# Adding the output projection's bias by an accumulating DMA instead of a thirteenth matmul

## The reference, cut to what matters

```python
qkv = x @ W_attn + b_attn
attn = softmax(masked(k q / sqrt(32)))        # 8 batches x 16 heads, 1024 x 1024
out = combine(attn, v)                        # 8 x 1024 x 512
x = layernorm(x + (out @ W_out + b_out))      # the part that changes: + b_out
scores = x @ w_router                         # top half of the tokens
x = layernorm(x + scatter(sigmoid(scores) * (gelu(x_sel @ W1 + b1) @ W2 + b2)))
```

## Time and profile before

| | |
|---|---|
| median of 3 runs | 2532.54 us (2531.82 to 2533.45) |
| span of the profiled execution | 2531.8 us; the page gives no time around it, the median is 0.7 above it |
| mean granted TensorE clock | 0.990 |
| PE busy | 2456.4 us (97%) |
| POOL busy | 1568.4 us (62%) |
| DVE busy | 1658.1 us (65%) |
| ACT busy | 1191.0 us (47%) |
| the attention alone, 127 to 1700 us | PE 1538.0 of 1573.0 us, POOL 1277.2, DVE 1149.2, ACT 943.9 |
| the feed-forward block, from 1860 us | PE 659.1 of 671.8 us, POOL 154.3 |

### The profile page before, as it was taken

One profiled execution on the slowest core, in us unless ns is written; L12 is line 12 of the kernel. 1 busy time (PEld: TensorE's weight loads), 2 busy tenths in 40 slices (PEclk: granted clock), 3 DMA queues, 4 the chain that ended last, 5 costly groups with the idle time before them and its releaser, 6 DMA issues. The chain is left out here.

```text
span 2531.8 us, 40908 instructions
## 1 busy us (share of the span) xinstructions
PE 2456.4 (97%) x14168; PEld 1817.1 (72%) x14168; DVE 1658.1 (65%) x4230; ACT 1191.0 (47%) x2035; POOL 1568.4 (62%) x1642
## 2 busy tenths in 40 slices
PE   8999999999999999999999999997999999999997
PEld 6656676767777677777767667774788888888886
DVE  7767677677767777767787776775655544553533
ACT  3665566556566656656656565566521111111110
POOL 2878778788888788878788887875233122221311
PEclk9999999999999999999999999998999999999999
DMA  4233445335344433535434343443421001010000
GB/s 175 89 127 120 146 141 195 123 127 182 125 147 158 153 134 136 172 131 177 146 124 159 123 172 128 158 146 102 162 80 35 24 26 43 25 34 26 26 25 17
DMA packets 167502, 287.45 MB, mean 114 GB/s; under 512 B 23241, under 2 KB 58121, under 8 KB 166026
## 3 DMA queue, kind: packets, MB, share of 16 engines
q1 hardware_dynamic: 160130, 267.99, 30.2%
q0 software_dynamic: 7168, 16.85, 2.1%
HBM read 116.97 MB, written 65.11 MB: 72 GB/s over the span
## 5 line engine op out<-in xcount | busy, mean ns | idle before, releaser
L867 POOL TENSOR_TENSOR Pa<-Pa,Pm 128x512 f32<-128x512 f32 (+1 forms) x602 | 744.8, 1262 | 105.8 <-ACT Pm L982 92.4
L1492 PE MATMUL PS<-Qp,Kp 128*128 128x512 f32 (+3 forms) x1536 | 488.8, 354 | 23.4 <-ACT Pm L982 13.1
L1458 PE MATMUL PS<-Kp,Qp 128*128 128x512 f32 (+3 forms) x1536 | 487.4, 352 | 9.1 <-DVE nm L1082 6.4
L982 ACT ACTIVATE Pm<-PS 128x512 f32<-128x512 f32 (+1 forms) x643 | 358.3, 569 | 264.7 <-PE PS L1492 219.4
L1082 DVE TENSOR_REDUCE nm<-PS 128x1 f32<-128x512 f32 x512 | 344.8, 688 | 188.0 <-PE PS L1458 187.7
L867 POOL TENSOR_TENSOR Pa<-Pa,P 128x512 f32<-128x512 f32 (+1 forms) x297 | 368.5, 1265 | 51.0 <-ACT P L982 44.4
L1458 PEld LDWEIGHTS PS<-Kp,Qp 128*128 128x128 f32 x1536 | 278.0, 190 | 110.0 <-issue 34.8
L1492 PEld LDWEIGHTS PS<-Qp,Kp 128*128 128x128 f32 x1536 | 278.0, 190 | 102.9 <-ACT Pa L982 28.9
L1090 DVE CUSTOM_DVE_ANT_0 PS<-PS,maskA 128x384 f32<-128x384 f32 (+3 forms) x512 | 246.4, 509 | 151.4 <-PE PS L1458 150.3
L944 ACT ACTIVATE G<-PS,b1c 128x512 f32<-128x512 f32 x128 | 88.2, 689 | 539.6 <-PE PS L1545 539.6
L1090 DVE CUSTOM_DVE_ANT_0 PS<-PS,maskA,nm 128x384 f32<-128x384 f32 (+3 forms) x512 | 265.1, 554 | 87.6 <-PE PS L1458 83.3
(11 more groups left out here) (149 smaller groups left out, 4229.2 us busy)
## 6 DMA issues: line engine op xcount, KB each, us to landing
Qp<-nat SPq DMA_DIRECT2D x192, 256.0 KB, 2.5
Kp<-nat SPq DMA_DIRECT2D x192, 256.0 KB, 2.9
o_s<-Of SPq DMA_DIRECT2D x64, 256.0 KB, 2.2
Ot<-o_s SPq DMA_DIRECT2D x64, 256.0 KB, 3.0
xb<-in_x SPq DMA_DIRECT2D x64, 256.0 KB, 3.0
h_s<-hs SPq DMA_DIRECT2D x64, 256.0 KB, 2.4
out<-xb SPq DMA_DIRECT2D x64, 256.0 KB, 2.4
x_raw<-in_xt SPq DMA_DIRECT2D x15, 1024.0 KB, 6.3
```

The lines of the kernel that those rows point to most:

```text
L867: e.tensor_tensor(to, to, probs(u, k)[:, h0:h0 + many, 0:w], ALU.add).then_inc(s["padd"], many)
L982: e.activation(probs(u, k)[:, hh[0]:hh[-1] + 1, 0:w], tile_bank(j)[:, 0:len(hh) * w].rearrange("p (h n) -> p h n", n=w), ACT.Exp).then_inc ...
L1458: ins = e.matmul(to, Qp[:, u % 4, h_, qt * P:qt * P + P], Kp[:, (2 * i + k0 // 512) % 4, h_, 0:w], start=True, stop=True)
L1492: ins = e.matmul(tile_bank(j)[:, x_ * w:x_ * w + w], Kp[:, (2 * i + k // 4) % 4, h_, k % 4 * P:k % 4 * P + P], Qp[:, u % 4, h_, 512 - w:51 ...
```

## The change

The thirteenth piece of O goes. CB becomes a full tile of 128 rows that all hold crow: once, after job C, SP stores crow to DRAM and loads it back to all partitions. For each O tile POOL issues one DMA that adds CB to xb in SBUF (128 x 512 float32, 256 KB), four beats after the load of xb at its place in the order, or one beat ahead of the tile's last piece where that is earlier. POOL waits for the load before it, DVE waits for it before line 1160. With 12 pieces T.beat of the O jobs 0 to 54 is one beat smaller, so that all that follows them in the order stands one beat earlier; for O number 55 to 63 it stays. The loads of xb keep their beats. SP's load of b2B, which reuses the memory, waits for all the additions.

```diff
-PIECES = {"K": [1] * 12, "Q": [1] * 12, "V": [1] * 12, "O": [1] * 13, ...
+PIECES = {"K": [1] * 12, "Q": [1] * 12, "V": [1] * 12, "O": [1] * 12, ...
-        CB = sb("CB", [P, D], F32R)
+        CB = sb("CB", [P, D], F32)
+        o_add = {}
+        for load in o_load:
+            for j in o_load[load]:
+                o_add.setdefault(min(load + 4, T.beat[j] - 1), []).append(j)
# sync
+                if n == T.beat["C",] + 2:
+                    e.wait_ge(*freed(("C",)))
+                    e.dma_start(cD[:, :], crow).then_inc(s["cb_st"], 16)
+                if n == T.beat["C",] + 5:
+                    e.wait_ge(s["cb_st"], 16)
+                    e.dma_start(CB[:, :], cD[0].rearrange("(a n) -> a n", a=1).broadcast_to([P, D])).then_inc(s["cb_in"], 16)
...
                     ff_load(7)
+                    for k in range(2):
+                        e.wait_ge(s["x_bias", k], 16 * len(T.o_jobs) // 2)
# gpsimd
-            e.memset(CB[:, :].bitcast(F32), 0.0).then_inc(s["ones"], 1)
...
                         layer_norm(o)
+                for j in o_add.get(n, ()):
+                    o = o_number(j)
+                    if o == 0:
+                        e.wait_ge(s["cb_in"], 16)
+                    e.wait_ge(s["xb", o % 2], 16 * (o // 2 + 1))
+                    e.dma_start(xb[:, o % 2, :], CB[:, :], accum_op=ALU.add).then_inc(s["x_bias", o % 2], 16)
# vector, job C
-                    link(e.tensor_tensor(crow, src[0:1, :], crow, ALU.add))
-                    linked()
-                    link(e.tensor_copy(CB[0:1, :], crow))
-                    linked()
-                    e.tensor_tensor(CB[96:97, :], crow, CB[0:1, :].bitcast(F32), ALU.subtract).then_inc(s["ev_v"], 1)
+                    e.tensor_tensor(crow, src[0:1, :], crow, ALU.add).then_inc(s["ev_v"], 1)
# vector, job O
-                    e.wait_ge(s["xb", o % 2], 16 * (o // 2 + 1))
+                    e.wait_ge(s["x_bias", o % 2], 16 * (o // 2 + 1))
# tensor, job O
-                    if k < 12:
-                        ins = e.matmul(to, Os[:, oh, kt, :], Wo[wh][:, kt, :], start=k == 0, stop=False)
-                    else:
-                        ins = e.matmul(to, ones[0:97, :], CB[0:97, :], start=False, stop=True)
+                    ins = e.matmul(to, Os[:, oh, kt, :], Wo[wh][:, kt, :], start=k == 0, stop=k == 11)
```

More of the change, by code:

```diff
@@ L157, in dense_jobs @@
     return jobs
-PIECES = {"K": [1] * 12, "Q": [1] * 12, "V": [1] * 12, "O": [1] * 13, "T": [2], "S": [1], "N": [4], "C": [4] * 4}
+PIECES = {"K": [1] * 12, "Q": [1] * 12, "V": [1] * 12, "O": [1] * 12, "T": [2], "S": [1], "N": [4], "C": [4] * 4}
 TICKS = 54
@@ L472, in layer @@
         bA, sc, sg = cs["battn"], cs["sc"], cs["sg"]
-        hD, scD, wD, oD = dr["h"], dr["sc"], dr["wqkv"], dr["o"]
+        hD, scD, wD, oD, cD = dr["h"], dr["sc"], dr["wqkv"], dr["o"], dr["cb"]
         xr = x.rearrange("b (t p) d -> b t p d", p=P)
@@ L1267, in vector @@
                     e.wait_ge(s["c0"], 9)
-                    e.wait_ge(s["ones"], 2)
+                    e.wait_ge(s["ones"], 1)
                     e.wait_ge(s["rk0"], 1)
@@ L1370, in wait_ready @@
                         e.wait_ge(s["wo_lo"], 2)
-                        e.wait_ge(*freed(("C",)))
                 if d >= 2:
@@ L1414, in dense @@
                 elif kind == "O":
-                    if k < 12:
-                        term, kt = divmod(k, KT)
-                        oh, wh = ((0, 0), (1, 0), (0, 1))[term]
-                        ins = e.matmul(to, Os[:, oh, kt, :], Wo[wh][:, kt, :], start=k == 0, stop=False)
-                    else:
-                        ins = e.matmul(to, ones[0:97, :], CB[0:97, :], start=False, stop=True)
+                    term, kt = divmod(k, KT)
+                    oh, wh = ((0, 0), (1, 0), (0, 1))[term]
+                    ins = e.matmul(to, Os[:, oh, kt, :], Wo[wh][:, kt, :], start=k == 0, stop=k == 11)
                 elif kind == "N":
@@ L1621 @@
 SEMAPHORES = ("c0", "bias", "b_scaled", "wq_in", "w1_in", "x0_hi", "rk0", "w_in", "w_hi", "w_split", "w_st", "v_in", "v_hi", "v_split", "v_st", "wo_in",
-              "wo_hi", "wo_lo", "x_hi", "x_lo", "ones", "rows", "d_mm", "ev_v", "ev_a", "kq_hi", "a_mm", "a_max",
+              "wo_hi", "wo_lo", "cb_st", "cb_in", "x_hi", "x_lo", "ones", "rows", "d_mm", "ev_v", "ev_a", "kq_hi", "a_mm", "a_max",
               "shift", "b_mm", "b_exp", "keep", "padd", "pv", "o_cp", "nln", "rinv", "ot", "os_hi", "os",
@@ L1626 @@
               "ghi", "glo", "dn", "q_clear", "k_ones")
-SLOTTED = {"xraw": 2, "of_st": 2, "nat": 2, "ost": 2, "hst": 2, "xb": 2, "lst": 2, "x0": 4, "rw": 8, "li": 2, "hg": 2, "fo": 4, "no_shift": 4}
+SLOTTED = {"x_bias": 2, "xraw": 2, "of_st": 2, "nat": 2, "ost": 2, "hst": 2, "xb": 2, "lst": 2, "x0": 4, "rw": 8, "li": 2, "hg": 2, "fo": 4, "no_shift": 4}
 def program(nc, x, xt, wqkv, wo, bat, b_out, w_router, W1, b1, W2, b2, out):
@@ L1635, in program @@
         "sc": nc.dram_tensor("sc_s", [B, N], F32).ap(),
+        "cb": nc.dram_tensor("cb_s", [1, D], F32).ap(),
         "o": nc.dram_tensor("o_s", [B, P, KT, N], F32).ap(),
```

## The result

The changed kernel takes 2667.55 us (median, 2665.16 to 2671.81) against 2532.76 us for the kernel before on the same chip: ratio 1.0532, 95% interval 1.0517 to 1.0547, 135 us slower. The prediction was 2563.5 us, with 2538 to 2595 as its range: the direction was right, and 104 us of the loss were not in it.

What follows compares the result with a forecast made beforehand. Bound: POOL's stretch, then PE's piece, in each attention pair. Matmuls -6.2 and -1.8, issues +30.0, ACT +4.9 and +2.7, tail +3.0 make +32.6, taken as +31 us: 2563.5 us, range 2538 to 2595.

Steps and rivals of the forecast that it cites:

- DVE, POOL and SP lose nothing: The order shifted one beat for 55 tiles: these three engines were put at no loss, ACT alone as different.
- rival 3: Accumulation lands late, DVE stalls from 9 us after the issue in odd slots; about 2650 us at 11 us; chance 0.06.
- another rule: A VectorE copy, cast or tensor_scalar all in SBUF keeps GpSimd's software descriptor generation out until it ends; sum left unchanged.
- The bound: Attention pair: POOL's stretch of additions and masks, 29.3 us, then 24.1 us in PE's piece; together 53.4 us.
- Rival 1: PE is the bound after all and all the matmuls are gained: -14.6 us, 2518 us; chance 0.08.
- The issue: POOL's issue of the accumulating DMA inside its stretch, odd slots: 1.11 us each, 27 times, 30.0 us lost.
- The sum for an ordinary pair: Attention pair without a new x split: 1.11 us issue, 0.23 us matmul gained, 0.1 us wait on ACT; period 54.3 us.
- ACT's order: Even slot: hs ahead of step 4's first exponential, 1.0 us, covered by POOL; with new x 0.7 us, 7 pairs, 4.9 us.
- the wait it named: Even slot: PE stalls 1.2 us instead of 0.18 for ACT's exponential, which waits until hs and xb are written.
- the small wait in the odd slot: hs comes ahead of one exponential in PE's piece; PE waits 0.1 us in each of 27 pairs, 2.7 us.
- The landing: DVE's wait for the accumulation, taken as 4 us: nothing for 55 tiles, 3.0 us lost in the tail.
- the load of x ahead of them: Tail: xb's load ahead of the bias DMA, taken as 3.0 us to land; DVE waits from tile 60 on alone.

Runs made afterwards that it cites:

- e5_gap: Changed kernel, whole, plus one wait: in step 5 of odd units POOL waits for its first addition before starting the second; 2571.8 us.
- e1: Changed kernel without its accumulating DMAs, bias left out, order still shifted by one beat; 2554.4 us.
- e11: Changed kernel without accumulating DMAs, bias left out; one POOL memset of CB in place of each odd-slot issue in the attention; 2550.3 us.
- e7: Changed kernel without accumulating DMAs, bias left out; two POOL memsets of CB in place of each odd-slot issue in the attention; 2557.7 us.
- e12: Changed kernel, whole; behind each odd-slot issue of the attention POOL also writes one column by memset and waits for it; 2563.9 us.
- e2: Changed kernel without accumulating DMAs, bias left out, no thirteenth matmul, in the order of the kernel before (13 ticks); 2522.9 us.
- e3: Changed kernel with its DMAs, the 12 matmuls spread over 13 ticks so the order is that of the kernel before; 2580.1 us.
- e10: Changed kernel without the accumulating DMA for the last ten tiles (54 to 63), whose bias is left out; 2659.3 us.
- e6: Changed kernel in the order of the kernel before, the attention's odd-slot xb loads earlier and their issues moved into POOL's pause; 2535.5 us.

## Why the prediction was wrong

**The step that failed** is the sentence "DVE, POOL and SP lose nothing", a term put at nothing. It looked at DVE for what moves in the order, not for what an issue of POOL, and a split one beat earlier beside it, do to DVE's instructions. An issue in POOL's stretch was priced as time of POOL alone. Its price was on DVE: a split with two SBUF inputs held, for up to five POOL instructions, in 20 of the 27 pairs, PE standing about 3 us for it, and the clock mostly at its lower level behind that. 96 of the 135 us (changed kernel against e5_gap). No rival had it; rival 3's 2650 us is near for another cause, and its sign, DVE idle behind the bias DMA in slots 11 to 63, is not in the trace.

The unit of the mechanism was in the Trainium skill, "SBUF — State Buffer", section "Who interferes with whom", the section the prediction cited for another rule: a DVE instruction with two SBUF inputs contends with a GpSimd instruction that reads SBUF, but not with one that only writes it. The traces agree that the split waits for the addition under way (0.9 to 1.7 us in e1, e11 and e5). They agree too that a memset, which only writes, doesn't keep it out (e7, e12). By the same page's section "SBUF: two separate sides" the one that starts first has the shared pair for the whole instruction, and the other is blocked; behind a DMA issue the runs show DVE held for five instructions, and there the measurement decides.

**The bound** was read rightly. In e2 the stretch is 29.32 us, the last step's matmul starts 0.15 us behind the mask, and only the odd slot's matmul counts, 0.23 us. Rival 1, all matmuls gained, needed 14.6 us less (2518); without any issue and any shift e2 is 7 to 14 us under the kernel before, at 2522.9.

**The issue** was over-priced: 1.11 us from the indirect DMA of the earlier trace rows; measured in e3 and in the changed kernel, the gap ahead of step 5 is 0.60 us instead of 0.14, so 0.46, although its record lasts 0.92: part of the record lies beside the additions on either side. 27 x 0.65 = 18 us too many.

**The sum for an ordinary pair** still came out: forecast +1.0 (1.11 - 0.23 + 0.1), measured in e5_gap +0.95. That is luck, errors against each other: in POOL's stretch 0.46 for the issue and 0.45 for the split that now pushes in between two additions (with the wait added in e5), in place of 1.11; and the other piece is 24.12 us instead of 24.10, so the matmul's 0.23 does not show there.

**ACT's order** had the right size by luck. Without the DMA (e1 against e2) the shift costs 54.2 - 53.2 = 1.0 us in an ordinary pair and 0.6 in one with new x, where the prediction had 1.0 and 0.7. But the wait it named is not there: ACT's exponential does come behind hs and xb, and PE stands for it 0.38 us in e1 and 0.44 in e2, not 1.2. What is new is a wait for DVE. With O's last piece one beat earlier, DVE's add to xb stands ahead of a row maximum (line 1092) that PE needs next. The same place in e1 and in e2:

```profile
1004.96 0.69 DVE L1166 TENSOR_TENSOR xb<-PS,xb 128x512 f32<-128x512 f32 x1 [0.21 <-PE PS L1422]
1006.30 1.27 DVE L1092 TENSOR_REDUCE nm<-PS 128x1 f32<-128x512 f32 x2
1007.12 0.27 PE L1467 MATMUL PS<-identf,nm 128*16 128x128 f32 x1 [0.55 <-DVE nm L1092]
```

```profile
989.45 0.69 DVE L1092 TENSOR_REDUCE nm<-PS 128x1 f32<-128x512 f32 x1 [0.22 <-PE PS L1460]
990.05 0.68 DVE L1166 TENSOR_TENSOR xb<-PS,xb 128x512 f32<-128x512 f32 x1
990.66 0.27 PE L1467 MATMUL PS<-identf,nm 128*16 128x128 f32 x1
```

Over the regular pairs up to 1166 us in e1 this wait comes 16 times, 10.9 us together, and not once in e2; PE's waits for ACT are 12.4 us there against 14.4. In a pair with new x it is 1.06 us, and the wait behind hs falls from 1.93 to 0.77 us. So "DVE loses nothing" failed here too. Of ACT's part only the small wait in the odd slot, forecast at 0.1 us, shows: 0.22. The prediction also missed the stretch from 1154 us to 1540 us in the kernel before (pairs 41 to 53), where DVE also counts the ranks: there e1 needs 398.3 us and e2 383.5, 2.1 us a pair. PE's waits for DVE's maxima are 11.7 us there in e1 against 3.9 in e2, and 3.5 us are the one held split; no run takes these apart further.

**The landing** was right in the attention (4.3 us median against the 4 taken, no wait of DVE before tile 58) and its cost too small in the tail. The term was 3.0 us. DVE waits 19.8 us there for the DMA, in tiles 58 to 63, and from tile 57 to 63 the changed kernel takes 57.9 us against 49.1; with no DMA there (e10) it is 46.2. What follows wins 2.7 back (681.0 against 683.7), and taking the DMAs out gives 8 us or somewhat more. The bias DMAs of these tiles land in 3.3 to 4.7 us, as taken. What the prediction had wrong is the load of x ahead of them: 3.0 us in its sum, but 7.0 us for tile 58 (5.6 in the kernel before), so the waits begin two tiles earlier than forecast.

In sum, from the medians, which were taken on several chips: matmuls about -10, shifted order +31.5, issues, one-addition waits and tail +17 (e5 against e1), held splits +96: 135. With the held splits away, the kernel is at 2571.8, inside the range given.

## What to carry to other kernels

An instruction added to one engine is not only its own time: look at which instructions of its neighbours stand near it, here VectorE's with two inputs in SBUF, and where they land once it is there. Put DMA issues of GpSimd right ahead of a point where it waits anyway, not into a run of its additions: in the order of the kernel before, that took the time from 2580 to 2535.5 us (e3 to e6). When a job moves in the order, ask what it now stands ahead of on every engine: here it was DVE's maxima. What an edit costs at its place in time depends on phases of a few tenths of a microsecond (one wait gave 96 us back), so a beat of shift belongs in the range of a forecast, not in a sentence that costs it at nothing.

## What the runs showed of the hardware

- A DVE tensor_tensor with both inputs in SBUF that starts late in a DMA issue of GpSimd, or inside the first addition right behind it (once the second), waits, in all but three places, for all the instructions that follow without a pause (4.85 us behind a plain DMA of one element, 5.1 behind the accumulating one); in the three it gets in after two additions (2.5 us). After a memset, or with nothing ahead, it gets in after one (0.9 to 1.6 us). A memset and a wait for it between issue and run gave 1.2 us in three places. Why an issue makes that difference stays open.
- An accumulating DMA of 256 KB from SBUF to SBUF: record of the issue 0.92 us, 0.46 us of delay for the instructions around it, 4.3 us median to landing. A plain one of one element: record 0.63 us, and still a gap of 0.59.
- PE standing 3.0 us was followed by 4 us at a granted clock of 0.57.
